# A cross-attention stage on one Trainium2 core: a two-slope pass on ScalarE in place of ramp and subtraction, and another order of TensorE's and ScalarE's work

## The reference, cut to what matters

```python
scores = einsum('bthd,bghd->bhtg', Q, K) / sqrt(32)
topv, topi = top_k(scores, 32)            # only the 32 largest of 2048 count
attn = zeros_like(scores).at[..., topi].set(softmax(topv))
c_t = einsum('btg,bgd->btd', attn.mean(heads), x_vision @ Wv)
x = layernorm(x) * (1 + gate * scale_in(c_t)) + gate * shift_in(c_t)
y = s4d(x)                                # long convolution by FFT
y = y * (1 + gate * scale_out(c_t)) + gate * shift_out(c_t)
```

## Time and profile before

| | us |
|---|---|
| median of 3 runs | 4655.69 (4653.27 to 4660.83) |
| profiled execution, its own time | 4659.99 |
| its span, first to last instruction | 4658.0 |
| cross stage within it (first to last score fold) | about 984 to 2984 |

### The profile page before, as it was taken

The page is one execution under the profiler, slowest core; times in us unless marked ns, Lnnn a source line. Parts: engine busy times, 40 slices in busy tenths (PEclk is TensorE's granted clock), DMA queues, the critical chain, the costliest instruction groups (busy, mean ns, idle before and its releaser), DMA issues. The chain is left out here.

```text
span 4658.0 us, 72037 instructions
## 1 busy us (share of the span) xinstructions
PE 4039.2 (87%) x28037; PEld 2944.3 (63%) x28066; DVE 3700.9 (79%) x4865; ACT 2070.8 (44%) x3816; POOL 2351.6 (50%) x2260
## 2 busy tenths in 40 slices
PE   8999995669999999999999999885788998999984
PEld 6777772336666676666766676674566666666652
DVE  5666666869999999999999999772577767766767
ACT  3334332125555555555554555412254454544543
POOL 1111113725666589998889988802333332333320
PEclk9999997769999999999999999897899999999997
DMA  2111114230111111121111111225411111112101
GB/s 84 53 49 46 53 44 166 75 117 28 37 37 51 45 39 42 46 64 30 42 51 63 38 30 39 89 73 181 139 48 52 49 50 53 51 47 61 46 23 38
DMA packets 216421, 276.08 MB, mean 59 GB/s; under 512 B 96899, under 2 KB 144707, under 8 KB 212560
## 3 DMA queue, kind: packets, MB, share of 16 engines
q1 hardware_dynamic: 198674, 216.92, 15.5%
q0 software_dynamic: 17408, 54.56, 3.2%
HBM read 186.44 MB, written 84.98 MB: 58 GB/s over the span
## 5 line engine op out<-in xcount | busy, mean ns | idle before, releaser
L1626 POOL TENSOR_TENSOR c_s<-c_s,c_z 128x2048 f32<-128x2048 f32 x128 | 581.4, 4542 | 358.3 <-ACT c_z L1382 352.0
L1956 PE MATMUL f_p_g<-f_hT,f_w 128*128 128x128 f32 x4096 | 537.6, 295 | 70.4 <-ACT f_gT L2056 55.9
L1192 PE MATMUL c_p_a<-c_diag,c_s 128*128 128x128 f32 x4096 | 526.0, 291 | 75.6 <-ACT c_diag L1396 67.0
L1192 PEld LDWEIGHTS c_p_a<-c_diag,c_s 128*128 128x128 f32 x4096 | 514.3, 207 | 111.7 <-ACT c_diag L1396 82.7
L1956 PEld LDWEIGHTS f_p_g<-f_hT,f_w 128*128 128x128 f32 x4096 | 526.1, 210 | 90.9 <-ACT f_gT L2056 58.8
L1964 PE MATMUL f_p_o<-f_w,f_gT 128*128 128x512 f32 x1024 | 481.8, 592 | 0.0
L1538 DVE TENSOR_TENSOR c_z<-c_s 128x1024 f32<-128x1024 f32 x256 | 456.6, 1783 | 3.7 <-ACT c_s L1371 3.7
L1263 PE MATMUL c_p_m<-c_wf,c_uT 128*128 128x512 f32 x768 | 383.4, 638 | 67.7 <-issue 63.3
L1371 ACT ACTIVATE c_s<-c_p_s 128x512 f32<-128x512 f32 x512 | 282.1, 590 | 293.7 <-PE c_p_s L1183 234.3
L1244 PEld LDWEIGHTS c_p_m<-c_aT,c_vals 128*128 128x128 f32 x3072 | 355.8, 194 | 62.5 <-issue 41.3
L1390 ACT ACTIVATE c_s<-c_s,c_nb 128x2048 f32<-128x2048 f32 x128 | 256.4, 2003 | 286.0 <-POOL c_s L1626 286.0
(11 more groups left out here) (378 smaller groups left out, 8900.9 us busy)
## 6 DMA issues: line engine op xcount, KB each, us to landing
mod_out<-c_fo POOLq DMA_DIRECT2D x32, 512.0 KB, 3.2
f_mr<-mod_out SPq DMA_DIRECT2D x32, 512.0 KB, 4.6
p_ct<-in_ctxT SPq DMA_DIRECT2D x16, 768.0 KB, 4.9
c_vals<-in_ctx SPq DMA_DIRECT2D x4, 3072.0 KB, 12.4
c_kb<-kspec SPq DMA_DIRECT2D x22, 512.0 KB, 5.0
a_xt<-in_xT SPq DMA_DIRECT2D x32, 256.0 KB, 3.2
a_xr<-in_x SPq DMA_DIRECT2D x32, 256.0 KB, 2.6
x<-a_out POOLq DMA_DIRECT2D x32, 256.0 KB, 2.5
```

Of the source, the lines that this page charges most:

```text
L1192: last = mm(p_a[:, n, :], s[:, j % RING, n * P:(n + 1) * P], diag[:, j % 2, :], start=(h == 0 and n % 4 == 0), stop=(h == NH2 - 1 and n % ...
L1626: pool.tensor_tensor(row, row, low, ALU.subtract).then_inc(cut_ready, 1)
L1956: last = mm(p_g[:, f % 8, :], w1[:, k, f * P:(f + 1) * P], hT[:, k * P:(k + 1) * P], start=(k == 0 and f % 4 == 0), stop=(k == KD - 1 and ...
```

## The change

For each head-row, ramp and subtraction become one pass in place: ScalarE applies the parametric ReLU with bias `-threshold` and the slope `STEEP` on the negative side to the score row. Scores over the threshold become `s - threshold`, those under it a very large negative number. GpSimd's `cut` is gone. `weigh` takes the bias from a new one-column tile `eb = SCALE * threshold - SCALE * max`, made by one more small instruction on ScalarE. VectorE gets one more small instruction, `floor(j)`: a `scalar_tensor_tensor` on 128 x 1 operands, both in SBUF, that keeps the threshold within 1024 of the maximum; `z_done` is now signalled by it, which stands behind the `max` of the next row's minimum, where before the last `max` of `top` signalled it. The tile loops of TensorE and of ScalarE are reordered: the score rounds stand in pairs, one directly behind the other.

```diff
             def below(j):
                 act.wait_ge(z_done, j + 1)
-                a(tb[:, par:par + 1], top[:, par, 31:32], ACT.Copy, scale=STEEP).then_inc(tb_ready, 1)
                 at_least(act, w_ready, j - 1)
+                a(tb[:, par:par + 1], top[:, par, 31:32], ACT.Copy, scale=-1.0).then_inc(tb_ready, 1)
                 a(nb[:, par:par + 1], top[:, par, 0:1], ACT.Copy, scale=-SCALE).then_inc(nb_ready, 1)
                 act.wait_ge(tb_ready, j + 1)
-                at_least(act, cut_ready, j)
-                a(low, s[:, j % RING, :], ACT.Relu, bias=tb[:, par:par + 1], scale=-STEEP).then_inc(low_ready, 1)
+                row = s[:, j % RING, :]
+                a(row, row, ACT.Prelu, bias=tb[:, par:par + 1], alpha=STEEP).then_inc(cut_ready, 1)
                 act.wait_ge(nb_ready, j + 1)
                 a(topx[:], top[:, par, :], ACT.Exp, bias=nb[:, par:par + 1], scale=SCALE,
                   accum_out=den[:, par:par + 1]).then_inc(sum_done, 1)
+                a(eb[:, par:par + 1], top[:, par, 31:32], ACT.Identity, bias=nb[:, par:par + 1], scale=SCALE).then_inc(eb_ready, 1)
 # weigh(j)
-                a(row, row, ACT.Exp, bias=nb[:, j % 2:j % 2 + 1], scale=SCALE).then_inc(w_ready, 1)
+                a(row, row, ACT.Exp, bias=eb[:, j % 2:j % 2 + 1], scale=SCALE).then_inc(w_ready, 1)
 # VectorE
+            def floor(j):
+                first, last = top[:, j % 2, 0:1], top[:, j % 2, 31:32]
+                v.scalar_tensor_tensor(last, first, -FAR, last, ALU.add, ALU.max).then_inc(z_done, 1)
...
-                    v.max(best[3], row).then_inc(z_done, 1)
-                    st.wait()
-                    st.mark(v.max(nxt[1], lower))
+                    st.behind(v.max(best[3], row))
+                    st.behind(v.max(nxt[1], lower))
+                    floor(j)
 # GpSimd: cut(j) and its four calls in each tile are gone
-            def cut(j):
-                pool.wait_ge(low_ready, j + 1)
-                row = s[:, j % RING, :]
-                pool.tensor_tensor(row, row, low, ALU.subtract).then_inc(cut_ready, 1)
```

More of the change, by code:

```diff
@@ L902, in cross @@
         RING = NH2 + 1
+        FAR = 1024.0
         TILES, LAST = TOK // P, TOK // P * NH2 - 1
@@ L971, in cross @@
         p_m = m.ps("p_m", [P, 2, 512])
-        (core_in, film_in, consts, values_in, s_done, s_copied, z_done, nb_ready, tb_ready, low_ready, cut_ready,
+        (core_in, film_in, consts, values_in, s_done, s_copied, z_done, nb_ready, tb_ready, eb_ready, cut_ready,
          sum_done, rd_ready, w_ready, im_ready, diag_ready, attn_done, aT_copied, uT_done, uT_copied,
@@ L979, in cross @@
             m.sem(n) for n in (
-                "core_in film_in consts values_in s_done s_copied z_done nb_ready tb_ready low_ready cut_ready "
+                "core_in film_in consts values_in s_done s_copied z_done nb_ready tb_ready eb_ready cut_ready "
                 "sum_done rd_ready w_ready im_ready diag_ready attn_done aT_copied uT_done uT_copied "
@@ L1290, in _ @@
                     spectra(t)
+                if slot_job(t) is not None:
+                    slot(t)
+                attn(j)
+                if t:
+                    context(t - 1, 0)
                 if more:
                     scores(t + 1, 0, 0)
[L1294 to L1299, removed]
                     scores(t + 1, 0, 1)
@@ L1302, in _ @@
                     context(t - 1, 1)
+                    context(t - 1, 2)
                 if more:
                     scores(t + 1, 0, 2)
-                if t:
-                    context(t - 1, 2)
-                if more:
                     scores(t + 1, 0, 3)
@@ L1445, in _ @@
                 more = t + 1 < TILES
+                if t > 1:
+                    copy_fi(t - 2)
                 if t:
                     below(j - 1)
-                if t > 1:
-                    copy_fi(t - 2)
                 copy_s(t, 1, 0)
+                copy_s(t, 1, 1)
                 if t:
@@ L1453, in _ @@
                     diagonal(j - 1)
-                copy_s(t, 1, 1)
                 if t > 1:
                     copy_fo(t - 2)
-                copy_s(t, 1, 2)
+                if more:
+                    copy_x(t + 1)
                 below(j)
                 if more:
-                    copy_x(t + 1)
+                    copy_q(t + 1)
                 if t:
                     copy_a(t - 1)
-                if more:
-                    copy_q(t + 1)
+                copy_s(t, 1, 2)
                 copy_s(t, 1, 3)
+                if forward_job(t) is not None:
+                    copy_f(t)
                 weigh(j)
                 diagonal(j)
-                if forward_job(t) is not None:
-                    copy_f(t)
+                if slot_job(t) is not None:
+                    copy_slot(t)
                 below(j + 1)
+                weigh(j + 1)
                 if more:
@@ L1475, in _ @@
                     copy_s(t + 1, 0, 1)
-                if slot_job(t) is not None:
-                    copy_slot(t)
                 diagonal(j + 1)
-                if more:
-                    copy_s(t + 1, 0, 2)
-                below(j + 2)
                 if t:
@@ L1485, in _ @@
                 if more:
+                    copy_s(t + 1, 0, 2)
                     copy_s(t + 1, 0, 3)
-                weigh(j + 1)
-                if not more:
-                    copy_fi(TILES - 2)
+                below(j + 2)
                 weigh(j + 2)
                 diagonal(j + 2)
+            copy_fi(TILES - 2)
             copy_fo(TILES - 2)
@@ L1548, in _ @@
                 best = [top[:, par, 8 * n:8 * n + 8] for n in range(4)]
-                at_least(dve, z_done, j)
                 st.link(fold(j, upper, ALU.max))
                 at_least(dve, sum_done, j - 1)
+                at_least(dve, eb_ready, j - 1)
                 st.link(v.max(best[0], row))
@@ L1570, in _ @@
                     st.link(v.match_replace(row, best[2], row, NEG))
-                    v.max(best[3], row).then_inc(z_done, 1)
+                    st.link(v.max(best[3], row))
+                    floor(j)
             invert(LAST)
```

12 lines of the change are left out of this document (4 added, 8 removed).

## The result

The changed kernel takes 5013.33 us (median of 4 runs, 5007.28 to 5018.21) against 4658.26 us for the kernel before in the same session. The ratio is 1.076, with a 95% interval of 1.074 to 1.078: 355 us slower. The forecast of slower held; its size, 4797 us, was far too small, and the time lies outside the range of 4645 to 4900.

A forecast was written before the change was run, and what follows sets the result against it. VectorE was taken to bound the kernel, TensorE close behind. Early tiles +41, late tiles +21 and TensorE's clock +75 us summed to +137 on the profiled 4660 us: 4797 us, range 4645 to 4900.

The forecast's parts named there:

- What bounds: Cross stage: VectorE, 99% busy, sets the pace before; after the change TensorE's loop with ScalarE does, VectorE at 90-96%.
- The waits of pairs and adjacent pieces: On TensorE, per late tile: 4.1 and 2.1 us of waits in paired rounds, 1.2 and 1.2 between adjacent pieces.
- TensorE's clock: TensorE's clock falling behind paired rounds: 2.6 us a tile taken, between 0 and 6.8; +75 us in 29 tiles.
- Cut removed: GpSimd without its cuts: no direct gain; 4.5 of the VectorE folds' 6.5 us excess a late tile kept.
- Floor: New small VectorE operation: 0.4 us a tile, plus 1.1 us a late tile waiting for GpSimd.
- Two-slope pass: ScalarE's pass replacing an equal ramp: 0 us, with the small `eb` instruction also 0.
- VectorE still bounds, and is relieved: Rival: TensorE's pair waits are absorbed and half the fold waits go, -59 us, 4601 us; chance 0.15.
- The rival of a table load: ScalarE needs two table loads of 1283 ns per head-row, +155 us on top, 4952 us; chance 0.04.
- that of the floor: Rival: VectorE's floors wait for GpSimd, folds aren't relieved, late tiles 2.5 us longer, 4712 us; chance 0.04.

The follow-up runs named there:

- the burst: Changed kernel plus 8 idle full-height products on TensorE behind the pair of blocks 2 and 3, ahead of spectra: 5022.15 us, ratio 1.077.
- two separate fills: Changed kernel with idle products only between the rounds of the pair of blocks 2 and 3 (4900.26 us), or only in the other three pairs (4901.94 us).
- the filled gap: Changed kernel plus 8 idle products ahead of spectra and 5 more in the wait between spectra and slot: 4941.16 us, ratio 1.060.
- the old order: Changed kernel's arithmetic with the TensorE and ScalarE tile loops in the order of the kernel before: 4580.2 us, ratio 0.983.
- all pairs filled: Changed kernel with idle full-height products between the two rounds of each pair, 9 in that of blocks 2 and 3, 5 in the others: 4784.58 us, ratio 1.027.
- the old arithmetic: Changed kernel's TensorE and ScalarE order with the ramp and cut of the kernel before and no floor: 5295.73 us, ratio 1.137.
- run 51: Not a run number: "that run" is the one with the old order, and 51 counts its floors that take more than 0.25 us.

## Why the prediction was wrong in its size, point by point

**What bounds.** VectorE before, TensorE with ScalarE's copies after: right. VectorE's share fell further than forecast (79%, forecast 90 to 96), and so did GpSimd's (47%, forecast some 65).

**The waits of pairs and adjacent pieces.** Right in place and size one by one: 3.84 us a short pair (forecast 3.9), 1.20 and 1.16 us between adjacent pieces (1.2 and 1.2). The long pair takes 5.47 us here, partly at the lower level; with the burst, where it ran at the high one, it takes 4.46 (2103.95 to 2108.41; forecast 4.6). Their sum was somewhat too large, by this estimate: between 1600 and 2970 us the trace shows 464 us at the lower level, and TensorE is busy for 439 of them. The lower level is half of the high one, so half of these 439 us is lost, 12.1 us for each tile of 75.6, so a late tile has 63.5 us without the clock's loss (forecast 64.9). From 1100 to 1600 us it is busy for 144 of 160 us, 10.3 us lost a tile, so an early tile has 61.1 (forecast 63.5).

**TensorE's clock: the step that failed.** The term "I take 2.6 us a tile" came to 12.1 us late and 10.3 early, by the estimate above. Both lie above even the bound of 6.8 us, which was four falls of 3.3 us with 1.7 us lost in each, as behind the pair of tile 9. That pair was followed by context products, and the level was high again after 3.3 us. In the new order the long pair is followed by spectra and slot, and there the level stayed low for 20.2 us. So the row was the nearest one for the pair, but not for what follows it, and the same length was taken for all falls. Over 31 tiles the clock's loss is some 360 us in place of the 75 forecast; without it a late tile would be 1.0 us shorter than before and an early one 2.3 longer, so that nearly the whole slowdown is the clock's by this estimate. What the runs show without an estimate is a lower bound: filling the waits within pairs recovered 229 us, two separate fills 113 and 111. The burst and the filled gap showed where the level falls and returns around spectra and slot; what it is in these two pieces that leaves the level low stays open. The page that I cited (TensorE: Matmul & The Clock Gate of the Trainium skill, section "What's actually happening") says that activity releases the throttle. Here TensorE was busy for 19.0 us of 20.2 and stayed throttled: the measurement decides.

**Cut removed.** Nothing direct and some relief of the folds: right in kind. I kept 4.5 of 6.5 us a tile; at 1226 against 1210 ns undisturbed, 8 folds keep 0.1 us in the changed kernel. With the old order they keep about 0.5 (1274 ns over the span). The relief was undersized, which cost the forecast nothing, since TensorE set the pace.

**Floor.** I took 1.5 us a tile. It measured 481 ns late in the changed kernel, 1.9 us a tile, which costs nothing there, since VectorE has room. With the old order, leaving it out together with its later signal gave 40 us in all.

**Two-slope pass.** Right: ScalarE has one table load in the cross stage, as before, and the pass costs what the ramp did (2002 ns, before 2003). ScalarE has 128 more instructions, the `eb` ones.

**The rivals.** "VectorE still bounds, and is relieved" at 4601 us is what the new arithmetic gives with the old order: 4580. It failed for the reason stated against it: the waits weren't absorbed. The rival of a table load would have shown two in each head-row, and that of the floor a VectorE that sets the pace; neither did.

**What stays open.** With all pairs filled the kernel is still 204 us above the one with the old order. The filling itself is a small part: the filled long pair takes 4.8 us (4.5 unfilled at the high level), one filled short pair 4.5 and the other two 3.9 (3.8 unfilled). The rest are the waits and the remaining fall in slot. No run parts these. The fills also change how often the level falls elsewhere (with the long pair filled, 52 stretches at the lower level between 1600 and 2970 us, but none over 10.3 us; 45 in the changed kernel, up to 20.5), so their 113 and 111 us say what each fill gives back, and not what a pair costs by itself.

## What to carry to other kernels

Before putting two short producers of one buffer side by side, count what the engine does while the buffer is copied; between longer pieces that copy cost nothing here, in a pair it stopped the engine. When a fall of TensorE's clock is priced from a row, look at what follows it and at how long the level stays low there: behind a pair with a wait of 0.8 us it cost 1.7 us ahead of context products, and behind one with a wait of 1.4 us some 10 us ahead of spectra and slot. And split a change that has an arithmetic and an ordering part: here the arithmetic gave -78 us with the old order, the order cost 433 us on top of it, and 638 us with the old arithmetic.

## What the runs showed of the hardware

- TensorE stayed at its lower level (0.50) for 20.2 us while it was busy for 19.0 of them, with spectra and slot. With idle products ahead of spectra, spectra took 3.7 to 4.5 us in 11 of 17 late tiles in place of 7.1; with idle products in the 1.2 us wait ahead of slot too, slot took 3.7 to 3.9 us in all of them.
- A VectorE operation with two SBUF inputs waits for GpSimd's running operation even at one element in each partition. The timeline of the old-order kernel (GpSimd ends at 2002.16, the floor at 2002.18):

```profile
2000.89 1.27 POOL L1684 TENSOR_TENSOR c_fw<-c_fz,c_ft 128x512 f32<-128x512 f32 x1
2001.46 0.72 DVE L1546 SCALAR_TENSOR_TENSOR c_top<-c_top 128x1 f32<-128x1 f32 x1
2002.10 1.21 DVE L1542 TENSOR_TENSOR c_z<-c_s 128x1024 f32<-128x1024 f32 x1
```

  So the rule of the Trainium skill (SBUF — State Buffer, section "SBUF: two separate sides") holds down to one element in each partition: 0.72 us here, 0.144 in the median of the 128. In that run 51 floors take more than 0.25 us, and each of them ends within 0.15 us of the end of a GpSimd operation.
- Idle products that nobody reads made a kernel 229 us faster.
